# Attention: Newton steps of the norms with fewer semaphore instructions, another wait for the product of k, and the copy of k ahead of its square

## The reference, cut to what matters

```
h = shift_token(x); q, k, v = split(h @ wqkv, 3)        # 8 heads of 64
q = q / clip(norm(q), 1e-12) * q_scale                   # norm over the 64 of a head
k = k / clip(norm(k), 1e-12) * k_scale
q, k = rotary_xpos(q, k)                                 # tables of cos and sin, times a scale
out = softmax(mask(8 * q @ k.T)) @ v                     # a window of the last 256 rows
x = x + out @ wo
```

## Time and profile before

| | us |
|---|---|
| median of 3 runs | 3240.29 (3239.17 to 3244.78) |
| the profiled execution, its own time | 3243.91 |
| its span, first to last instruction | 3241.7 |
| TensorE busy | 3088.7 (95%) |
| VectorE busy | 1820.4 (56%) |
| ACT busy | 1490.1 (46%) |
| GpSimd busy | 1028.4 (32%) |

### The profile page before, as it was taken

One profiled execution on the slowest core, in us unless ns is written; L12 is line 12 of the kernel. 1 busy time (PEld: TensorE's weight loads), 2 busy tenths in 40 slices (PEclk: granted clock), 3 DMA queues, 4 the chain that ended last, 5 costly groups with the idle time before them and its releaser, 6 DMA issues.

```text
span 3241.7 us, 48323 instructions
## 1 busy us (share of the span) xinstructions
PE 3088.7 (95%) x16534; PEld 2565.0 (79%) x16534; DVE 1820.4 (56%) x3933; ACT 1490.1 (46%) x3198; POOL 1028.4 (32%) x1670
## 2 busy tenths in 40 slices
PE   9997999999977999999998999999995999999999
PEld 8986888888866788888877888888874788887887
DVE  4655777777765333333324777777775434333332
ACT  2116888888861111111113888888883111111111
POOL 0316555665536000000044565556555100000000
PEclk8999999999988999999999999999997999999999
DMA  4421111111123111101131111111104201111110
GB/s 150 139 77 33 62 61 66 66 66 56 56 59 114 40 40 40 37 3 40 39 119 40 56 66 56 66 66 66 53 27 137 74 14 53 46 52 53 52 39 20
DMA packets 149779, 194.50 MB, mean 60 GB/s; under 512 B 23286, under 2 KB 90998, under 8 KB 149284
## 3 DMA queue, kind: packets, MB, share of 16 engines
q1 hardware_dynamic: 133700, 175.69, 16.3%
q10 hardware_dynamic: 15840, 15.73, 1.5%
HBM read 120.06 MB, written 41.95 MB: 50 GB/s over the span
## 4 chain that ended last, share of the span: by engine, by line
PE 76%; POOL 12%; issue 6%; DVE 3%; ACT 3%; POOLq 0%; DVEq 0%; SPq 0%; ACTq 0%
PE bank L343 21%; PE bank L345 21%; PE bank L344 21%; PE bank L578 4%; PE bank L812 3%; PE bank L774 3%; POOL a_tmp L1634 2%; POOL a_krot L1636 2%; PE bank L791 2%; POOL a_rt L1606 1%; POOL a_rs L1609 1%; DVE a_krot L1314 1%; POOL a_rt L1605 1%; POOL a_rt L1608 1%; ACT a_sq L1011 1%
## 5 line engine op out<-in xcount | busy, mean ns | idle before, releaser
L1171 ACT ACTIVATE f_gate<-bank,f_b 128x512 f32<-128x512 f32 (+1 forms) x176 | 121.2, 689 | 998.8 <-PE bank L345 998.8
L343 PE MATMUL bank<-f_hT_hi,f_w_hi 128*128 128x512 f32 (+1 forms) x1408 | 556.8, 395 | 15.6 <-ACT f_hT_hi L1152 14.3
L1514 DVE SCALAR_TENSOR_TENSOR f_uraw<-bank,f_b,f_gate 128x512 f32<-128x512 f32 (+1 forms) x176 | 132.0, 750 | 752.5 <-ACT f_gate L1171 752.3
L345 PE MATMUL bank<-f_hT_hi,f_w_lo 128*128 128x512 f32 (+1 forms) x1408 | 553.2, 393 | 0.0
L344 PE MATMUL bank<-f_hT_lo,f_w_hi 128*128 128x512 f32 (+1 forms) x1408 | 552.6, 392 | 0.0
L343 PEld LDWEIGHTS bank<-f_hT_hi,f_w_hi 128*128 128x128 f32 (+1 forms) x1408 | 261.1, 185 | 77.8 <-ACT f_hT_hi L1152 15.0
L1066 ACT ACTIVATE a_P<-a_S,a_bias 128x384 f32<-128x384 f32 x512 | 310.1, 611 | 6.6 <-DVE a_bias L1349 6.2
L345 PEld LDWEIGHTS bank<-f_hT_hi,f_w_lo 128*128 128x128 f32 (+1 forms) x1408 | 260.9, 185 | 64.2
L344 PEld LDWEIGHTS bank<-f_hT_lo,f_w_hi 128*128 128x128 f32 (+1 forms) x1408 | 261.1, 185 | 62.6
L1349 DVE CUSTOM_DVE_ANT_0 a_S<-bank,a_masks,a_q 128x384 f32<-128x384 f32 x512 | 295.6, 615 | 26.2 <-PE bank L774 20.7
L1059 ACT ACTIVATE a_P<-a_P,a_inv 128x384 f32<-128x384 f32 x512 | 287.2, 612 | 2.1 <-DVE a_inv L1355 0.5
(11 more groups left out here) (165 smaller groups left out, 6552.2 us busy)
## 6 DMA issues: line engine op xcount, KB each, us to landing
a_h<-x_layer_in SPq DMA_DIRECT2D x128, 128.0 KB, 2.7
a_res<-x_layer_in SPq DMA_DIRECT2D x64, 256.0 KB, 2.8
x_after_attention<-out_tiles SPq DMA_DIRECT2D x64, 256.0 KB, 2.0
f_res<-x_after_attention SPq DMA_DIRECT2D x64, 256.0 KB, 3.2
f_stage<-in_L_ffn_w SPq DMA_DIRECT2D x60, 256.0 KB, 3.4
a_V<-a_V SPq DMA_DIRECT2D x28, 512.0 KB, 5.2
f_h<-x_after_attention ACTq DMA_DIRECT2D x28, 512.0 KB, 4.2
c_x<-in_x SPq DMA_DIRECT2D x32, 256.0 KB, 2.8
```

What stands on the lines that cost most here:

```text
L343: pe.matmul(dst, w[0], m[0], start=start, stop=False)
L345: return pe.matmul(dst, w[1], m[0], start=False, stop=stop)
L1514: dve.scalar_tensor_tensor(f_uraw[0:ROWS[m], m % 2, :], bank[pair_of(u, m, end)][0:ROWS[m], :], f_b1[0:ROWS[m], 0, m:m + 1], f_gate[0:ROWS ...
```

## The change

- `k_copy` waits for k's projection itself and stands ahead of `square(1, ...)`, in the loop and in the head.
- `k_norm` waits for the last Newton step (`a_rs_step`), no longer for `a_norms_set`, which line 1611 signals.
- In `norms` the sum is multiplied by -0.5 in the first operation already, the integer constant is adapted to it, and the Newton step's third operation becomes a tensor_tensor that adds a column of 1.5, read 16 times; its `waits_end` is gone. The column is a new tensor ahead of all others but two, set once at the start behind a new semaphore.

```
+RSQRT_SEED_OF_NEGATIVE_HALF = RSQRT_SEED - float(1 << 30) - float(1 << 22)
...
         out_tiles = sb("out_tiles", [P, 2, D])
+        three_halves = sb("three_halves", [P, 1])
...
                 def k_copy(x):
+                    act.wait_ge(a_k_mm, START + G + x + 1)
                     act.wait_ge(a_k_rotated, START + G + x)
...
                 def head_k():
                     h_T(1)
+                    k_copy(0)
                     square(1, 0)
-                    k_copy(0)
...
                         if here(t + 2):
+                            k_copy(t + 2)
                             square(1, t + 2)
-                            k_copy(t + 2)
...
                 def k_norm(x):
-                    dve.wait_ge(a_norms_set, START + G + x + 1)
+                    dve.wait_ge(a_rs_step, START + (G + x + 1) * NORM_STEPS)
...
-                    step(0, base, pool.tensor_scalar(a_ss[:], a_ss[:], 1e-24, None, ALU.max))
+                    step(0, base, pool.tensor_scalar(a_ss[:], a_ss[:], 1e-24, -0.5, ALU.max, ALU.mult))
                     waits_end(pool)
-                    step(1, base, pool.tensor_scalar(a_rs[:].bitcast(I32), a_ss[:].bitcast(I32), -0.5, RSQRT_SEED,
+                    step(1, base, pool.tensor_scalar(a_rs[:].bitcast(I32), a_ss[:].bitcast(I32), -0.5, RSQRT_SEED_OF_NEGATIVE_HALF,
                                                      ALU.mult, ALU.add))
                     for i in range(3):
                         step(2 + 4 * i, base, pool.tensor_tensor(a_rt[:], a_rs[:], a_rs[:], ALU.mult))
                         step(3 + 4 * i, base, pool.tensor_tensor(a_rt[:], a_rt[:], a_ss[:], ALU.mult))
-                        waits_end(pool)
-                        step(4 + 4 * i, base, pool.tensor_scalar(a_rt[:], a_rt[:], -0.5, 1.5, ALU.mult, ALU.add))
+                        step(4 + 4 * i, base, pool.tensor_tensor(a_rt[:], a_rt[:], three_halves[:].to_broadcast([P, 2 * H]), ALU.add))
                         step(5 + 4 * i, base, pool.tensor_tensor(a_rs[:], a_rs[:], a_rt[:], ALU.mult))
...
             pool.sem_inc(started, 1)
+            pool.memset(three_halves[:], 1.5).then_inc(three_halves_set, 1)
+            pool.wait_ge(three_halves_set, START + 1)
```

More of the change, by code:

```diff
@@ L227, in adaln_ffn_program @@
         waits_over = {eng.engine: sem(f"waits_over{i}") for i, eng in enumerate((nc.sync, nc.tensor, nc.vector, nc.gpsimd))}
-        ident_in = sem("ident_in"); zero_set = sem("zero_set"); pads_out = sem("pads_out")
+        ident_in = sem("ident_in"); three_halves_set = sem("three_halves_set"); zero_set = sem("zero_set"); pads_out = sem("pads_out")
         c_cond_in = sem("c_cond_in"); c_q_in = sem("c_q_in"); c_bk_in = sem("c_bk_in"); c_bias_in = sem("c_bias_in"); c_wq_in = sem("c_wq_in"); c_wk_in = sem("c_wk_in")
```

## The result

The changed kernel takes 3185.65 us (median; 3183.29 to 3189.56, 4 runs), the kernel before 3240.53 beside it. The ratio is 0.983, with a 95% interval of 0.9813 to 0.9847: 1.7% or 55 us faster. The forecast was 3186 us, with 3180 to 3203 as the range. The profiled execution took 3186.28 us, its span is 3184.1.

What follows compares the result with a forecast made beforehand. A closed loop through k's chain was taken to bound each tile, with TensorE next; 60 x 0.85 = 51.0, plus 2.5 and 0.7, gives 54.2 us off the median 3240.29, so 3186 us, range 3180 to 3203.

Steps and rivals of the forecast that it cites:

- closed loop: Steady tile: k's projection, ACT, GpSimd, VectorE's product, k's transposes and back to the next projection, one period of 21.49 us.
- TensorE's hole: TensorE's loss at k's transposes in each steady tile, put at 0.85 us, more than the 0.63 of busy time.
- Part 1: ACT copies k ahead of squaring it: 0.50 us out of the loop, at cost 0.
- Part 2: GpSimd's Newton steps: 0.70 us becomes 0.60 in each of three steps, 0.30 us in all.
- rival C: GpSimd's add with the repeated column takes a slow path, 0.75 us each: 23 us slower, 3263 us; chance 0.04.
- Part 3: VectorE's product for k starts after the last Newton operation, not line 1611: 0.43 us earlier.
- The ceiling: TensorE becomes the limit of a steady tile: of 1.23 us cut, only 0.85 land.
- The slack forecast: The part of the 1.23 us cut from a steady tile's chain that brings no time: 0.38 us.
- The sum: Steady tiles 51.0 us, tile 1 of both layers 2.5, tile 0 of the first layer 0.7: 54.2 us.
- upside: Shorter stalls may leave TensorE's clock at 2.4 GHz: 1.7 us more, as much or a bit more at layer 0's tile 0.
- A: GpSimd's line 1611 beats k's product to the shared ports, margin 0.1 us: gain some 46 us, 3194 us; chance 0.16.
- B: Another VectorE or ACT wait takes the hole's place, smallest margin 0.28 us: gain 29 us, 3211 us; chance 0.10.

Runs made afterwards that it cites:

- wait_only: Kernel before with only the wait of k's product moved to the last Newton step: 3215.23 us, ratio 0.9909.
- copy_first: Kernel before with only ACT's order changed, k's copy ahead of its square: 3215.49 us, ratio 0.9911.
- two_more_adds: Changed kernel with two more 16-column GpSimd operations between the last Newton step and the product's wait: 3205.71 us, ratio 0.9879.
- copy_and_wait: Kernel before with the copy ahead and the product's new wait, Newton steps as before: 3184.5 us, ratio 0.9815.
- whole_change: The changed kernel run again, unaltered, beside three other runs on one chip: 3184.58 us, ratio 0.9824 to the kernel before.
- late_product: Changed kernel with three small VectorE reciprocals in front of k's product, so GpSimd's line for q's factors starts first: 3184.57 us, ratio 0.9814.
- wide_op_first: Changed kernel with the three reciprocals and a 256-column GpSimd multiply behind the last Newton step, not waited for by the product: 3205.77 us, ratio 0.9888.
- newton_only: Kernel before with only the Newton steps changed, k's product waiting for line 1611 as before: 3229.04 us, ratio 0.9952.

## Why the prediction was right

**The bound.** The closed loop with TensorE's hole at k's transposes was right: wait_only and copy_first moved the whole tile by nearly what they take out of the chain.

**Part 1, the copy.** Forecast 0.50 us, alone it gave 0.47 a tile. The square, 0.5 us later, cost nothing.

**Part 2, the Newton steps.** Forecast 0.30. From the first to the last start they take 4.04 instead of 4.32 us, as the first operation with its second stage is 0.28 long where it had been 0.25; alone they gave 0.24 a tile. That a second stage costs nothing was wrong by 0.03 us. The add with the repeated column is 0.22, as taken, and rival C is out. That the semaphore instruction made the 0.42 is argued and not shown: it stood only ahead of tensor_scalars, and the change took away both at once, so the form of the operation is a rival that no run here separates from it.

**Part 3, the wait.** Forecast 0.43, alone it gave 0.37 to 0.41.

**The ceiling.** This was the step that carried the number. The hole was put at 0.85 us from start to start, against 0.64 in brackets, and a tile became 0.86 shorter. Taken by the idle time alone the gain would have been 60 x 0.64 + 3 = 41 us, too little by 14. The slack forecast was 0.38, the profile has 0.35 and two_more_adds shows 0.34. copy_and_wait shows what follows and what the prediction did not spell out: the Newton part brings nothing in a steady tile once the other two are in.

**The sum.** 60 x 0.86 = 51.6 us (forecast 51.0). First tiles: tile 0 of the first layer waits 0.71 less (6.72 to 6.01; forecast 0.73). Tile 1 of the first layer waits longer, 2.04 instead of 1.62: TensorE reaches it sooner as it ran faster in between. The clock shows in two stretches, k's transposes and the projection of tile 0, first the kernel before, then the changed one:

```profile
257.17:263.01 5.84, 5.84 (x17) 4.69 (x17) 1.24 (x2) 0.60 (x1) 2.90 (x4) 0.52 0.00 0
```

```profile
256.36:260.96 4.60, 4.60 (x16) 3.83 (x17) 1.23 (x2) 0.60 (x1) 3.68 (x5) 0.68 0.00 0
```

At a mean of 0.68 instead of 0.52 the same work takes 1.24 us less. It was named as an upside and not counted (a granted clock of 0.5 is the level of 1.2 GHz, 1.0 that of 2.4). With 0.8 before it and 1.2 behind (tile 1's 1.23) it makes up the 3.24 us to the first mark. In the second layer the clock was low at another place instead, in a projection to v ahead of tile 1's transposes:

```profile
1737.04:1740.77 3.73, 3.73 (x13) 2.92 (x11) 1.31 (x4) 3.40 (x8) 2.82 (x11) 0.54 0.00 0
```

So little came back there, and TensorE came later to tile 1, which is part of why its wait fell from 3.23 to 0.46, by more than the 1.23 cut out of the chain. The sum was 54.2 us. The medians here differ by 54.9, the two profiled executions by 57.6, and the medians beside whole_change by 58. That the forecast met its median within 1 us is therefore in part luck; what the reasoning gave is the 51.6 us of the steady tiles, and about 3 us around them vary with the clock and with the execution.

**Rivals.** A's margin was put at 0.1 us and is 0.15, and VectorE won; but A's price was wrong. A line of 8 columns 0.06 us ahead of the product does not hold it up (late_product), so a race lost by that little would have cost nothing; it is a wide operation that does (wide_op_first). The Trainium skill's rule (SBUF — State Buffer, "SBUF: two separate sides") of an exclusive lock for whoever starts first agrees here in which of two operations is held up, 1.14 against 0.69 us for the product behind a wide operation and 0.65 against 0.24 for the 8 columns behind the product. It does not agree with late_product, where the 8 columns started first by their rows and the product kept its 0.67. B did not come: ACT's margin was put at 0.28 and is 0.40.

Each part alone gives 0.02 to 0.06 us less than its forecast cut. The rows account for it: copy_first takes 0.49 us out ahead of GpSimd's rotation, newton_only 0.28 out of the steps, wait_only 0.42 out ahead of the product, and TensorE's own stretch, from k's transposes to the last pass of k's projection, is 10.14 us before and in copy_first, but 10.17 in newton_only and 10.14 to 10.17 in wait_only. What stays open is why that stretch grows by 0.03, whether it was the semaphore instruction or the form of the operation that made the 0.42, and what sets the places at which the clock falls.

## What to carry to other kernels

When one engine waits a little in every turn of a loop, follow the chain from its last product back to its wait: if it closes, its length is the loop's, and every cut counts until the hole is gone. Measure the hole from start to start against a turn without the wait, not by the idle time, and work out which of several cuts fill it; the rest is slack. Of two signals that an engine sends in a row, let the one that is urgently waited for be tested by itself.

## What the runs showed of the hardware

- A GpSimd operation of 16 columns takes 0.22 us and the next starts 0.30 us behind it, waiting for its semaphore; with one more semaphore instruction between them and a tensor_scalar as the next one it is 0.42. Reading one column 16 times costs nothing extra (0.22 us).
- Whether a VectorE product of two SBUF operands or the GpSimd operation beside it became longer went by order and size: 0.65 instead of 0.24 us for 8 columns started 0.15 us behind the product, nothing for either when these 8 columns started 0.06 us ahead, 1.24 instead of 0.73 for 256 columns started 0.05 behind it, 1.14 instead of 0.69 for the product when 256 columns started 0.14 ahead of it.
- TensorE lost 0.86 us a tile where its rows show 0.64 idle, and 0.26 where they show none (two_more_adds).
